# The ternary feed-forward of a two-layer network: its row parts and gelu outputs as two float32r parts instead of three bf16 parts, its square roots on GpSimd, its row normalisation on VectorE

## Chip, cores and metric

The kernel runs on one core of a Trainium2 chip. Times are device microseconds (us) of the whole kernel. The kernel before takes 2742.81 us, the median of 3 runs (2739.74 to 2743.94).

## What is computed

Sixteen sequences ("rows" of the work, b = 0 to 15) of 512 tokens and 256 features go through two layers, each an attention and a feed-forward with a residual. The change touches the last of the four stages, the ternary feed-forward, and the few lines at the end of the stage ahead of it that prepare its first row:

```python
def _ternary_linear(x, w):
    alpha = jnp.mean(jnp.abs(w))
    w_t = jnp.sign(w) * (jnp.abs(w) > 0.5 * alpha).astype(w.dtype)   # -1, 0 or 1
    rms = jnp.sqrt(jnp.sum(x * x, axis=-1, keepdims=True)) / jnp.sqrt(d)
    return jnp.einsum('bsd,fd->bsf', x / (rms + EPS), w_t)
h = jax.nn.gelu(_ternary_linear(layernorm(x), w_up), approximate=False)   # 256 -> 1024
x = x + _ternary_linear(h, w_down)                                        # 1024 -> 256
```

## The kernel before

One program for five engines, each with its own instruction order, tied by semaphores. The first attention ("ratio"), the low-rank feed-forward and the second attention ("zeroed") come first; `ternary_feed_forward` starts after all engines have met at the end of the second attention.

In this last stage x stays in SBUF. The work is 16 rows of `FC` = 8 slots; slot n is row b = n // 8 and block f = n % 8 of 128 hidden features, for all 512 tokens. The ternary weights lie in SBUF as bf16, where -1, 0 and 1 are exact. Float precision of the other operand comes from splitting it: a value is the sum of three bf16 parts, and a product is three bf16 matmuls that accumulate in one PSUM bank.

- **TensorE** (`pe`): `up(n)` does 2 feature halves x 3 parts = 6 matmuls with 512 moving columns (line 2237) into one of `H_BANKS` = 3 banks; `down(n)`, issued `T_LAG` = 3 slots later, does 4 token tiles x 3 parts = 12 matmuls (line 2248) whose stationary operand is a 128x128 tile of a gelu part and whose 256 moving columns are the weights. `turn_x` (line 119) transposes two token tiles of the next row in slots f = 1 and 4 (`T_TURN_AT`), 4 float32 transposes each, into the one `prep_bank`; `row_sums` (line 2259) in slot f = 7 adds the squares of the row before over partitions, into the same bank.
- **ScalarE** (`act`): in each slot `gelu` (2289, in place in PSUM), `high_part` (2294, the first bf16 part), `square` (2306). Beside them `keep_x` and `middle_x` (2280, 2285: parts 0 and 1 of the next row's x), once a row a square root for the hidden scale (2325), and once the roots for the late rows (2309, 2310). The root's function table and gelu's are loaded in turn, so each root costs two table loads.
- **VectorE** (`dve`): in each slot `split_rest` (2343: bank minus part 0), `split_mid` (2349: part 1) and `split_low` (2353: part 2). Beside them `split_x` (2336), `hidden_scale` (2359, 2361), and `finish` (2367), which adds a row's result to x in slots 0 and 1 of the row two later.
- **GpSimd** (`pool`): `normal` (2411: the next row's x normalised, two tiles at a time, at f = 0 and 2), the running sum of squares (2428, seven a row), `low_x` (2418: part 2 of x).

An up is released by the x parts of its row and by the bank of slot n - 3 being read (`h_rest`); a down by `h_lo`; a first down of a row by `x_added`, the finished x of the row two before, since down banks alternate in two pairs:

```python
q.wait_ge(s["h_rest"], n - H_BANKS + 1)                                # up(n)
q.wait_ge(s["h_lo"], n + 1)                                            # down(n)
q.wait_ge(s["x_added"], added(b - 2) if b >= 2 else 0)                 # down(n)
```

## Time and profile before

| | us |
|---|---|
| median of 3 runs (2739.74 to 2743.94) | 2742.81 |
| profiled execution, span from first to last instruction | 2743.6 |
| TensorE matmul busy in it | 2603.3 (95%) |
| VectorE, ScalarE, GpSimd busy | 2281.0, 2078.9, 1812.7 |

For the profiled execution the span is the only time that is shown; it lies 0.8 us over the median and inside the three runs. Lengths below are differences within this span. Busy shares are means over four stages of different kinds; the stage that the change touches is the last 377 us. Matmuls are pipelined, so the "mean ns of one" of a matmul includes the way through the array, and the distance between starts says what one costs in a stream.

### The profile page before, as it was taken

What the parts mean: (1) busy time and instruction counts of PE and PEld (TensorE: products, weight loads), DVE (VectorE), ACT (ScalarE), POOL (GpSimd) and SP (SyncE); (2) the same over time, 40 slices, a digit from 0 to 9 for tenths busy, and PEclk for the clock granted to TensorE, in tenths of its full rate; (3) what the DMA queues carried; (4) which work ended last, traced back from release to release, by engine and by line L of the source; (5) the groups of instructions that cost most, each with busy time, mean ns of one, the idle gap of its engine ahead of it and who ended that gap; (6) DMA issues with size and microseconds to landing.
All of it is one profiled execution on the core that took longest, in us unless ns stands there. A gap on an engine that the chain in (4) does not pass through costs nothing. (4 is left out here: it accounts for less than half of the span.)

```text
span 2743.6 us, 75250 instructions
## 1 busy us (share of the span) xinstructions
PE 2603.3 (95%) x27002; PEld 1814.6 (66%) x27044; DVE 2281.0 (83%) x6935; ACT 2078.9 (76%) x3788; POOL 1812.7 (66%) x3152
## 2 busy tenths in 40 slices
PE   5999999999999999999889999999999999899999
PEld 3777777777777777777333367777777767567666
DVE  5999999999999999988555588888888888599998
ACT  4998999998989999998334367677667676578886
POOL 4767666776677677766331177777777777578885
PEclk8999999999999999999989999999999999899999
DMA  4334433443343244322100256565655553000001
GB/s 121 72 60 76 76 61 63 81 81 63 63 81 71 54 75 81 70 49 46 41 1 20 50 100 104 97 101 99 104 102 99 101 96 66 1 16 24 24 24 39
DMA packets 110387, 182.21 MB, mean 66 GB/s; under 512 B 27008, under 2 KB 96384, under 8 KB 97920
## 3 DMA queue, kind: packets, MB, share of 16 engines
q1 hardware_dynamic: 106176, 175.82, 34.5%
q8 instruction: 216, 3.54, 0.6%
q10 hardware_dynamic: 3840, 1.58, 0.3%
q14 instruction: 155, 1.27, 0.2%
HBM read 116.25 MB, written 60.29 MB: 64 GB/s over the span
## 5 line engine op out<-in xcount | busy, mean ns | idle before, releaser
L922 POOL TENSOR_TENSOR ratio_scores<-ratio_scores,ratio_max_cols 128x512 f32<-128x512 f32 (+3 forms) x1024 | 726.3, 726 | 318.9 <-DVE ratio_max_cols L807 317.6
L198 PE MATMUL bank<-ratio_k_stack,ratio_q_stack 102*128 102x512 bf16 (+7 forms) x2048 | 506.1, 303 | 32.9 <-DVE ratio_max_cols L807 18.6
L1486 DVE CUSTOM_DVE_ANT_0 zeroed_unused<-bank,zeroed_drop 128x512 bf16<-128x512 f32 (+3 forms) x1024 | 439.7, 484 | 107.6 <-PE bank L198 107.6
L807 DVE CUSTOM_DVE_ANT_0 ratio_scores<-bank,ratio_scores 128x512 f32<-128x512 f32 (+3 forms) x1024 | 472.5, 489 | 22.2
L1362 ACT ACTIVATE arena<-bank 128x512 f32<-128x512 f32 x640 | 370.4, 593 | 150.3 <-PE bank L1255 148.9
L656 ACT ACTIVATE ratio_prob<-bank 128x512 f32<-128x512 f32 x640 | 378.8, 592 | 103.9 <-PE bank L554 101.1
L797 DVE TENSOR_TENSOR ratio_scores<-bank,ratio_inverse 128x512 f32<-128x512 f32 x640 | 435.9, 681 | 16.3 <-PE bank L198 9.6
L551 PE MATMUL bank<-const_f_sb,ratio_scores 128*128 128x128 f32 x2560 | 410.0, 274 | 0.9 <-ACT ratio_prob L656 0.9
L645 ACT ACTIVATE ratio_inverse<-bank 128x512 f32<-128x512 f32 x640 | 381.1, 596 | 12.0 <-PE bank L201 12.0
L649 ACT ACTIVATE ratio_inverse<-ratio_inverse 128x1024 f32<-128x1024 f32 x320 | 338.7, 1058 | 10.1
L1621 POOL TENSOR_SCALAR_AFFINE_SELECT arena<-arena 128x256 f32<-128x256 f32 (+1 forms) x640 | 227.9, 362 | 164.3 <-ACT arena L1362 159.9
L551 PEld LDWEIGHTS bank<-const_f_sb,ratio_scores 128*128 128x128 f32 x2560 | 301.6, 141 | 42.1 <-issue 1.9
L198 PEld LDWEIGHTS bank<-ratio_k_stack,ratio_q_stack 96*128 96x128 bf16 (+1 forms) x2048 | 179.0, 98 | 192.6 <-DVE ratio_max_cols L807 110.5
L1255 PE MATMUL bank<-zeroed_q_stack,zeroed_k_stack 99*128 99x128 bf16 x2560 | 249.8, 219 | 11.5 <-ACT arena L1362 10.8
L198 PE MATMUL bank<-zeroed_k_stack,zeroed_q_stack 96*128 96x512 bf16 (+3 forms) x1024 | 248.0, 305 | 2.8 <-PEq L2163 2.1
L1255 PEld LDWEIGHTS bank<-zeroed_q_stack,zeroed_k_stack 99*128 99x128 bf16 x2560 | 178.1, 97 | 91.3 <-ACT arena L1362 56.0
L554 PE MATMUL bank<-const_b_sb 128*128 128x128 bf16 x1024 | 211.9, 219 | 0.0
L2428 POOL TENSOR_TENSOR ternary_square_sum<-ternary_square_sum,ternary_squares 128x512 f32<-128x512 f32 x112 | 151.0, 1348 | 73.4 <-ACT ternary_squares L2306 70.7
L201 PE MATMUL bank<-const_b_sb 128*128 128x128 bf16 x1024 | 193.1, 220 | 0.0
L2248 PE MATMUL bank<-ternary_w_down_T,ternary_h_parts 128*128 128x256 bf16 x1536 | 189.1, 273 | 2.2 <-DVE ternary_h_parts L2353 2.2
L1961 ACT ACTIVATE lowrank_hidden<-bank,lowrank_b 128x512 f32<-128x512 f32 x128 | 82.2, 685 | 135.0 <-PE bank L1843 135.0
L2248 PEld LDWEIGHTS bank<-ternary_w_down_T,ternary_h_parts 128*128 128x128 bf16 x1536 | 150.3, 98 | 47.8 <-DVE ternary_h_parts L2353 4.3
(223 smaller groups left out, 5436.3 us busy)
## 6 DMA issues: line engine op xcount, KB each, us to landing
ratio_q_stack<-ratio_parts_q SPq DMA_DIRECT2D x186, 128.0 KB
ratio_k_stack<-ratio_parts_k SPq DMA_DIRECT2D x186, 128.0 KB
zeroed_q_stack<-zeroed_parts_q SPq DMA_DIRECT2D x186, 128.0 KB, 4.5
zeroed_k_stack<-zeroed_parts_k SPq DMA_DIRECT2D x186, 128.0 KB, 7.4
ratio_parts_q<-arena SPq DMA_DIRECT2D x96, 128.0 KB
ratio_parts_k<-arena SPq DMA_DIRECT2D x96, 128.0 KB
zeroed_parts_q<-shared_parts SPq DMA_DIRECT2D x96, 128.0 KB
zeroed_parts_k<-shared_parts SPq DMA_DIRECT2D x96, 128.0 KB
```

The source lines that it names most:

```text
L198: i = e.matmul(bank[:, off:off + w], qs[0:rows, s, hh, ib * P:(ib + 1) * P], ks[0:rows, s, hh, 0:w], start=(k == 0), stop=mask is None, sk ...
L551: e.matmul(bank[:, at], scores[:, n % S_BUFS, at], net.ident, is_transpose=True, start=first, stop=False, skip_group_check=True)
L645: e.activation(inv[:, n % INV_BUFS, :], shared("denoms", n)[:, :], ACT.Ln, scale=-2.0, bias=EPS_RATIO).then_inc(s["log_den"])
L649: e.activation(both, both, ACT.Exp, scale=-1.0).then_inc(s["inverse"])
L656: e.activation(prob[:, n % PROB_BUFS, 0:wd], exp_banks[n % 2][:, 0:wd], ACT.Exp).then_inc(s["prob"])
L797: e.tensor_tensor(scores[:, n % S_BUFS, 0:wd], dot_banks[n % 2][:, 0:wd], inv[:, n % INV_BUFS, 0:wd], ALU.mult).then_inc(s["weighed"])
L807: i = e.tensor_tensor_reduce(seg, dot_banks[n % 2][:, at], seg, 1.0, 0.0, ALU.mult, ALU.max, mx[:, pair % M_BUFS, c:c + 1])
L922: i = e.tensor_tensor(seg, seg, mx[:, pair % M_BUFS, c:c + 1].to_broadcast([P, w]), ALU.subtract)
L1255: i = e.matmul(bank[:, off + jb * P:off + (jb + 1) * P], ks[0:STACK + FOLD_ROWS, st, hh, jb * P:(jb + 1) * P], qs[0:STACK + FOLD_ROWS, st, ...
L1362: e.activation(prob[:, n % FOLD_PROBS, 0:wd], exp_banks[n % 2][:, 0:wd], ACT.Exp, scale=0.25).then_inc(s["prob"])
L1486: i = e.tensor_tensor_reduce(unused[:, n % 2, at], bank[:, at], drop[:, L - (ib + 1) * P:L], 1.0, 0.0, ALU.add, ALU.max, mx[:, pair % FOLD ...
L2248: i = e.matmul(banks[t // 2][:, (t % 2) * D:(t % 2 + 1) * D], h_parts[:, n % H_BUFS, part, t * P:(t + 1) * P], ternary.down[:, f, :], star ...
```

## The change

In the last stage every three-part bf16 product becomes a two-part float32r product: x parts and h parts are float32r tensors `[P, 2, 2, L]` and `[P, H_BUFS, 2, L]`; an up is 4 matmuls, a down 8. The weights are copied once, at the start of the stage, from bf16 to float32r: eight copies by VectorE (`up_w`), eight by GpSimd (`down_w`). The middle parts and the rests go away; VectorE's part of a slot is one subtraction (`low_part`). VectorE also takes `normal` (from GpSimd) and `keep_x` (from ScalarE). The square roots are GpSimd's `pow` with 0.5, after a small VectorE operation that reads PSUM (`hidden_mean`); ScalarE keeps gelu, high part and square. `finish` and `hidden_scale` go to slots 0 and 1. The last bank wait of an up is now for `h_lo` and `h_squared`. At the end of the stage ahead, the first row's x is split in two parts instead of three. Of the diff, without the functions that only changed engine or were removed:

```diff
-        self.parts = sb("shared_parts", [P, 2, 3, L], BF16)
-        self.rest = sb("shared_rest", [P, L])
-        self.x_parts = self.parts[:, :, :, :].rearrange("p a b t -> p (a b t)").rearrange("p (k c t) -> p k c t", k=3, c=2)
-        self.x_rest = self.rest[:, :].rearrange("p (c t) -> p c t", c=2)
+        sb("shared_block", [P, 4 * L])
+        base = nc.sbuf_base - 16 * L
+        self.parts = nc.alloc_sbuf_tensor_at("shared_parts", [P, 2, 3, L], BF16, offset=base)
+        self.rest = nc.alloc_sbuf_tensor_at("shared_rest", [P, L], F32, offset=base + 12 * L)
+        self.x_parts = nc.alloc_sbuf_tensor_at("ternary_first_parts", [P, 2, 2, L], F32R, offset=base)
...
-            def first_rest(pair):
+            def first_low(pair):
                 q.wait_ge(ts["x_hi"], pair + 1)
-                q.wait_ge(ts["x_lo"], pair)
                 q.wait_ge(s["lo"], 2 * halves)
-                e.tensor_tensor(rows.x_rest, prep_bank[:, :].rearrange("p (c t) -> p c t", c=2), x_part(pair, 0),
-                                ALU.subtract).then_inc(ts["x_rest"])
+                e.tensor_tensor(x_part(pair, 1), prep_bank[:, :].rearrange("p (c t) -> p c t", c=2), x_part(pair, 0),
+                                ALU.subtract).then_inc(ts["x_lo"])
...
-        xn, x_rest = start.xn, start.x_rest
-        x_parts = (start.x_parts, sb("x_parts", [P, 3, 2, L], BF16))
-        h_parts = sb("h_parts", [P, H_BUFS, 3, L], BF16)
-        h_rest = sb("h_rest", [P, 2, L])
+        up_w = sb("up_wide", [P, 2, F], F32R)
+        down_w = sb("down_wide", [P, FC, D], F32R)
+        xn = start.xn
+        x_parts = (start.x_parts, sb("x_parts", [P, 2, 2, L], F32R))
+        h_parts = sb("h_parts", [P, H_BUFS, 2, L], F32R)
         sq = sb("squares", [P, 2, L])
         total = sb("square_sum", [P, 2, L])
         hs = sb("h_scale", [P, 2, T])
+        half = sb("half", [P, B * T - start.rows])
...
             def turn_x(b, pair):
                 q.wait_ge(s["xn"], 2 * b + pair + 1)
-                q.wait_ge(s["x_rest"], 2 * b + pair)
+                q.wait_ge(s["x_lo"], 2 * b + pair)
                 if pair == 0:
-                    q.wait_ge(s["h_rms"], b - 2)
+                    q.wait_ge(s["h_mean"], b - 2)
                 turn_blocks(e, prep_bank, lambda t: xn[:, t % 2, :], pair, net.ident).then_inc(s["turned"])
 
             def up(n):
                 b, f = divmod(n, FC)
+                if b == 0:
+                    q.wait_ge(s["up_wide"], f + 1)
                 q.wait_ge(s["x_lo"], 2 * b + 2)
-                q.wait_ge(s["h_rest"], n - H_BANKS + 1)
+                q.wait_ge(s["h_lo"], n - H_BANKS + 1)
+                q.wait_ge(s["h_squared"], n - H_BANKS + 1)
                 for c in range(2):
-                    for part in range(3):
-                        i = e.matmul(h_banks[n % H_BANKS][:, :], ternary.up[:, c, f * P:(f + 1) * P], x_parts[b % 2][:, part, c, :],
-                                     start=(c == 0 and part == 0), stop=(c == 1 and part == 2))
+                    for part in range(2):
+                        i = e.matmul(h_banks[n % H_BANKS][:, :], up_w[:, c, f * P:(f + 1) * P], x_parts[b % 2][:, part, c, :],
+                                     start=(c == 0 and part == 0), stop=(c == 1 and part == 1))
                 i.then_inc(s["up"])
 
             def down(n):
                 b, f = divmod(n, FC)
                 banks = down_banks[2 * (b % 2):2 * (b % 2) + 2]
+                if b == 0:
+                    q.wait_ge(s["down_wide"], f + 1)
+                q.wait_ge(s["h_hi"], n + 1)
                 q.wait_ge(s["h_lo"], n + 1)
                 q.wait_ge(s["x_added"], added(b - 2) if b >= 2 else 0)
                 for t in range(T):
-                    for part in range(3):
+                    for part in range(2):
                         i = e.matmul(banks[t // 2][:, (t % 2) * D:(t % 2 + 1) * D],
-                                     h_parts[:, n % H_BUFS, part, t * P:(t + 1) * P], ternary.down[:, f, :],
-                                     start=(f == 0 and t % 2 == 0 and part == 0), stop=(f == FC - 1 and part == 2),
+                                     h_parts[:, n % H_BUFS, part, t * P:(t + 1) * P], down_w[:, f, :],
+                                     start=(f == 0 and t % 2 == 0 and part == 0), stop=(f == FC - 1 and part == 1),
                                      skip_group_check=True)
                 i.then_inc(s["down"])
...
             def row_sums(b):
                 q.wait_ge(s["h_summed"], (b + 1) * (FC - 1))
-                q.wait_ge(s["h_rms"], b)
-                q.wait_ge(s["x_rest"], min(2 * (b + 3), 2 * B))
+                q.wait_ge(s["h_mean"], b)
+                q.wait_ge(s["x_lo"], min(2 * (b + 3), 2 * B))
                 for t in range(T):
...
-            for n in range(n_slots + FC):
-                b, f = divmod(n, FC)
-                if n < n_slots:
-                    gelu(n)
-                    high_part(n)
-                    square(n)
-                if b + 1 < B and f in T_TURN_AT:
-                    keep_x(b + 1, T_TURN_AT.index(f))
-                if b + 1 < B and f in T_PARTS_AT:
-                    middle_x(b + 1, T_PARTS_AT.index(f))
-                if b and f == T_SUMS_AT:
-                    q.wait_ge(s["h_rows"], b)
-                    q.wait_ge(s["x_added"], added(b - 3) if b >= 3 else 0)
-                    e.activation(hs[:, (b - 1) % 2, :], prep_bank[:, 0:T], ACT.Sqrt, scale=1.0 / F).then_inc(s["h_rms"])
-                if n == ROOTS_AT:
-                    roots()
+            for n in range(n_slots):
+                gelu(n)
+                high_part(n)
+                square(n)
...
+            def keep_x(b, pair):
+                q.wait_ge(s["turned"], 2 * b + pair + 1)
+                q.wait_ge(s["up"], (b - 1) * FC)
+                e.tensor_copy(x_part(b, pair, 0), prep_bank[:, :].rearrange("p (c t) -> p c t", c=2)).then_inc(s["x_hi"])
+
             def low_x(b, pair):
-                q.wait_ge(s["x_mid"], 2 * b + pair + 1)
-                q.wait_ge(s["up"], (b - 1) * FC)
-                e.tensor_tensor(x_part(b, pair, 2), x_rest[:, :, :], x_part(b, pair, 1), ALU.subtract).then_inc(s["x_lo"])
-
-            for n in range(n_slots):
+                q.wait_ge(s["x_hi"], 2 * b + pair + 1)
+                e.tensor_tensor(x_part(b, pair, 1), prep_bank[:, :].rearrange("p (c t) -> p c t", c=2), x_part(b, pair, 0),
+                                ALU.subtract).then_inc(s["x_lo"])
+
...
+            def low_part(n):
+                q.wait_ge(s["h_hi"], n + 1)
+                q.wait_ge(s["h_squared"], n + 1)
+                e.tensor_tensor(h_parts[:, n % H_BUFS, 1, :], h_banks[n % H_BANKS][:, :], h_parts[:, n % H_BUFS, 0, :],
+                                ALU.subtract).then_inc(s["h_lo"])
+
+            def hidden_mean(b):
+                q.wait_ge(s["h_rows"], b + 1)
+                e.tensor_scalar(hs[:, b % 2, :], prep_bank[:, 0:T], 1.0 / F, None, ALU.mult).then_inc(s["h_mean"])
+
...
+            for f in range(FC):
+                e.tensor_copy(up_w[:, :, f * P:(f + 1) * P], ternary.up[:, :, f * P:(f + 1) * P]).then_inc(s["up_wide"])
+            for n in range(n_slots + 2 * FC):
                 b, f = divmod(n, FC)
+                if n < n_slots:
+                    low_part(n)
                 if b + 1 < B and f in T_XN_AT:
                     normal(b + 1, T_XN_AT.index(f))
-                if f:
+                if b + 1 < B and f in T_KEEP_AT:
+                    keep_x(b + 1, T_KEEP_AT.index(f))
+                    low_x(b + 1, T_KEEP_AT.index(f))
+                if 0 < b <= B and f == T_SUMS_AT:
+                    hidden_mean(b - 1)
+                if n == SCALES_AT:
+                    scales()
+                if 2 <= b < B + 2 and f == 0:
+                    hidden_scale(b - 2)
+                if 2 <= b < B + 2 and f < 2:
+                    finish(b - 2, 2 * f)
+                    finish(b - 2, 2 * f + 1)
+
...
+            def roots():
+                variance = net.mean_var[:, start.rows:B * T, 1]
+                e.tensor_scalar(scale[:, :], variance, 1e-5, None, ALU.add).then_inc(s["std_in"])
+                q.wait_ge(s["halves"], 1)
+                e.tensor_tensor(rms[:, :], variance, half[:, :], ALU.pow).then_inc(s["std"])
+                q.wait_ge(s["std_in"], 1)
+                e.tensor_tensor(scale[:, :], scale[:, :], half[:, :], ALU.pow).then_inc(s["std"])
+
+            def hidden_root(b):
+                out = hs[:, b % 2, :]
+                q.wait_ge(s["h_mean"], b + 1)
+                q.wait_ge(s["halves"], 1)
+                e.tensor_tensor(out, out, half[:, 0:T], ALU.pow).then_inc(s["h_rms"])
+
+            e.memset(half[:, :], 0.5).then_inc(s["halves"])
+            for f in range(FC):
+                e.tensor_copy(down_w[:, f, :], ternary.down[:, f, :]).then_inc(s["down_wide"])
+            for n in range(n_slots + FC):
+                b, f = divmod(n, FC)
+                if n < n_slots and f:
                     q.wait_ge(s["h_squared"], n + 1)
                     if f > 1:
                         q.wait_ge(s["h_summed"], summed(n) - 1)
                     e.tensor_tensor(total[:, b % 2, :], total[:, b % 2, :], sq[:, n % 2, :], ALU.add).then_inc(s["h_summed"])
-                if b + 1 < B and f in T_PARTS_AT:
-                    low_x(b + 1, T_PARTS_AT.index(f))
+                if b and f == T_SUMS_AT:
+                    hidden_root(b - 1)
+                if n == ROOTS_AT:
+                    roots()
```

TensorE's order from the row sums at the end of row 1 to the first transposes (`L119`) in slot 1 of row 2. Before:

```order
L2259 MATMUL bank<-const_f_sb,ternary_square_sum 128x1 x4
L2237 MATMUL bank<-shared_parts,ternary_w_up_T 128x512 x6
L2248 MATMUL bank<-ternary_w_down_T,ternary_h_parts 128x256 x12
L2237 MATMUL bank<-shared_parts,ternary_w_up_T 128x512 x6
L2248 MATMUL bank<-ternary_w_down_T,ternary_h_parts 128x256 x12
L119 MATMUL bank<-const_f_sb,shared_xn 128x128 x4
```

Now, at the same place (`L120` is the same helper one line later, `ternary_first_parts` the x parts of even rows):

```order
L2255 MATMUL bank<-const_f_sb,ternary_square_sum 128x1 x4
L2230 MATMUL bank<-ternary_first_parts,ternary_up_wide 128x512 x4
L2244 MATMUL bank<-ternary_down_wide,ternary_h_parts 128x256 x8
L2230 MATMUL bank<-ternary_first_parts,ternary_up_wide 128x512 x4
L2244 MATMUL bank<-ternary_down_wide,ternary_h_parts 128x256 x8
L120 MATMUL bank<-const_f_sb,shared_xn 128x128 x4
```

The order of ups, downs and transposes stays; only the number of matmuls in each falls by a third.

VectorE's order in slots 0 to 2 of row 12. Before (`L2343`, `L2353`, `L2349` are the three splits of gelu's output, the middle one of them for the slot before):

```order
L2343 TENSOR_TENSOR ternary_h_rest<-bank,ternary_h_parts 128x512
L2353 TENSOR_TENSOR ternary_h_parts<-ternary_h_rest,ternary_h_parts 128x512
L2349 CAST ternary_h_parts<-ternary_h_rest 128x512
L2367 SCALAR_TENSOR_TENSOR x<-bank,ternary_h_scale,x 128x256 x2
L2343 TENSOR_TENSOR ternary_h_rest<-bank,ternary_h_parts 128x512
L2353 TENSOR_TENSOR ternary_h_parts<-ternary_h_rest,ternary_h_parts 128x512
L2349 CAST ternary_h_parts<-ternary_h_rest 128x512
L2367 SCALAR_TENSOR_TENSOR x<-bank,ternary_h_scale,x 128x256 x2
```

Now, from the low part of slot 0 (`L2326`) on; `L2309` normalises two token tiles of row 13, `L2316` and `L2320` are their two parts, `L2344` is `finish`:

```order
L2326 TENSOR_TENSOR ternary_h_parts<-bank,ternary_h_parts 128x512
L2309 TENSOR_SCALAR shared_xn<-x,mean_var,ternary_x_scale 128x256 x2
L2336 TENSOR_SCALAR ternary_h_scale<-ternary_h_scale 128x4
L2338 RECIPROCAL ternary_h_scale<-ternary_h_scale 128x4
L2344 SCALAR_TENSOR_TENSOR x<-bank,ternary_h_scale,x 128x256 x2
L2326 TENSOR_TENSOR ternary_h_parts<-bank,ternary_h_parts 128x512
L2344 SCALAR_TENSOR_TENSOR x<-bank,ternary_h_scale,x 128x256 x2
L2326 TENSOR_TENSOR ternary_h_parts<-bank,ternary_h_parts 128x512
L2309 TENSOR_SCALAR shared_xn<-x,mean_var,ternary_x_scale 128x256 x2
L2316 CAST ternary_x_parts<-bank 128x2x256
L2320 TENSOR_TENSOR ternary_x_parts<-bank,ternary_x_parts 128x2x256
```

A slot of VectorE has one operation instead of three, and the normalisations, which were GpSimd's, now stand behind the low parts of slots 0 and 2. GpSimd's order per row is seven sums of squares and one `pow`.

## Rows read from the trace of the kernel before

**Rows 1.** Head of the page: span, and busy time of each engine.
```profile
span 2743.6 us, 75250 instructions
PE 2603.3 (95%) x27002; PEld 1814.6 (66%) x27044; DVE 2281.0 (83%) x6935; ACT 2078.9 (76%) x3788; POOL 1812.7 (66%) x3152
```
**Rows 2.** Busy time by windows: stretch, length, each engine, clock, DMA share, GB/s.
```profile
2366.60:2413.10 46.50, 42.08 (x263) 27.17 (x269) 36.13 (x48) 31.47 (x56) 34.77 (x25) 0.93 0.00 1
...
2435.90:2731.80 295.90, 292.52 (x2050) 206.19 (x2083) 266.04 (x419) 238.22 (x402) 235.69 (x164) 1.00 0.07 24
```
**Rows 3.** Waits of PE from 2413 us on: total, times, longest.
```profile
PE bank L2248 <- DVE ternary_h_parts L2353: 1.3, 2, 1.1
PE bank L2237 <- POOL ternary_x_parts L2418: 1.3, 3, 0.9
```
**Rows 4.** Timeline of PE, a steady slot: start, length, engine, line, operation, count.
```profile
2590.15 1.47 PE L2248 MATMUL bank<-ternary_w_down_T,ternary_h_parts 128*128 128x256 bf16 x12
2591.46 1.46 PE L2237 MATMUL bank<-ternary_x_parts,ternary_w_up_T 128*128 128x512 bf16 x6
2592.75 1.47 PE L2248 MATMUL bank<-ternary_w_down_T,ternary_h_parts 128*128 128x256 bf16 x12
```
**Rows 5.** Timeline of PE: the first and the fifteenth of the sixteen row sums.
```profile
2413.12 0.95 PE L2259 MATMUL bank<-const_f_sb,ternary_square_sum 128*128 128x1 f32 x8
...
2731.84 0.95 PE L2259 MATMUL bank<-const_f_sb,ternary_square_sum 128*128 128x1 f32 x8
```
**Rows 6.** Timeline of PE in earlier stages: float32 products and transposes.
```profile
300.91 1.94 PE L576 MATMUL bank<-ratio_w_o,arena 128*128 128x256 f32 x8
...
1291.49 0.60 PE L563 MATMUL bank<-const_f_sb,ratio_o_group 128*128 128x128 f32 x4
```
**Rows 7.** One line's instructions, ns min/median/max: weight loads, float32 and bf16.
```profile
L525 PEld LDWEIGHTS bank<-ratio_w_in,arena x512: 186/192/333, 27.1 to 1244.0; 128*128 128x128 f32 x171
...
L2248 PEld LDWEIGHTS bank<-ternary_w_down_T,ternary_h_parts x1536: 95/98/181, 2374.7 to 2736.8; 128*128 128x128 bf16 x192
```
**Rows 8.** Timeline of ACT where it runs without a wait.
```profile
2417.91 0.59 ACT L2306 ACTIVATE ternary_square_sum<-bank 128x512 f32<-128x512 f32 x1
2418.39 0.60 ACT L2289 ACTIVATE bank<-bank 128x512 f32<-128x512 f32 x1
2419.02 0.60 ACT L2294 ACTIVATE ternary_h_parts<-bank 128x512 bf16<-128x512 f32 x1
2419.52 0.59 ACT L2306 ACTIVATE ternary_squares<-bank 128x512 f32<-128x512 f32 x1
```
**Rows 9.** Timeline around one slot: down, next gelu, square, subtraction.
```profile
2502.04 1.47 PE L2248 MATMUL bank<-ternary_w_down_T,ternary_h_parts 128*128 128x256 bf16 x12
2502.24 0.58 ACT L2289 ACTIVATE bank<-bank 128x512 f32<-128x512 f32 x1 [0.91 <-PE bank L2237]
...
2503.35 0.59 ACT L2306 ACTIVATE ternary_squares<-bank 128x512 f32<-128x512 f32 x1
...
2504.08 0.68 DVE L2343 TENSOR_TENSOR ternary_h_rest<-bank,ternary_h_parts 128x512 f32<-128x512 f32 x1
```
**Rows 10.** Groups by line and shape: busy us, mean ns of one.
```profile
L2343 DVE TENSOR_TENSOR ternary_h_rest<-bank,ternary_h_parts 128x512 f32<-128x512 f32 x128 | 87.7, 685 | 42.5 <-ACT ternary_square_sum L2306 31.4 <-ACT ternary_squares L2306 6.2 <-issue 3.6
L2367 DVE SCALAR_TENSOR_TENSOR x<-bank,ternary_h_scale,x 128x256 f32<-128x256 f32 x64 | 27.7, 477 | 0.0
L1988 DVE COPY lowrank_xn_T<-bank 128x512 f32<-128x512 f32 x16 | 11.0, 690 | 15.8 <-PE bank L119 15.8
L1456 DVE TENSOR_SCALAR shared_xn<-x,mean_var,rstd 128x256 f32<-128x256 f32 x60 | 24.3, 448 | 0.0
L1601 POOL TENSOR_SCALAR zeroed_neg_max<-zeroed_max_cols 128x8 f32<-128x8 f32 x128 | 31.6, 247 | 6.4 <-DVE zeroed_max_cols L1486 6.4
L2428 POOL TENSOR_TENSOR ternary_square_sum<-ternary_square_sum,ternary_squares 128x512 f32<-128x512 f32 x112 | 151.0, 1348 | 73.4 <-ACT ternary_squares L2306 70.7
```
**Rows 11.** Timeline, start of the stage: first up, first transposes.
```profile
2367.09 3.71 PE L2237 MATMUL bank<-shared_parts,ternary_w_up_T 128*128 128x512 bf16 x11 [2.50 <-PEq L1695]
...
2370.64 0.60 PE L119 MATMUL bank<-const_f_sb,shared_xn 128*128 128x128 f32 x4
```
**Rows 12.** Timeline, end of the stage: the last root and the last finish.
```profile
2738.00 0.17 ACT L2325 ACTIVATE ternary_h_scale<-bank 128x4 f32<-128x4 f32 x1 [4.08 <-PE bank L2259]
...
2738.62 1.66 DVE L2367 SCALAR_TENSOR_TENSOR x<-bank,ternary_h_scale,x 128x256 f32<-128x256 f32 x4
```

90 lines of the change are left out of this document (22 added, 68 removed).

## Prediction

> **What bounds the kernel now.** I read the head of the page first [rows 1]: TensorE is busy 95% of the span and no other engine over 83%. That is a mean over four stages, so the second view is the busy time by windows for the stage that the change touches [rows 2]: from 2435.90 to 2731.80 us, thirteen of its rows, TensorE's matmuls are busy 292.5 of 295.9 us, VectorE 266, ScalarE 238, GpSimd 236, at the full clock (granted 1.00, the 2.4 GHz level). Third, TensorE's waits from 2413 us on [rows 3]: they sum to about 3 us. So in this stage TensorE is the bound by its own work, and every other engine waits for it.
>
> What a slot costs is read from starts [rows 4]: down starts at 2590.15, up at 2591.46, down at 2592.75. So 12 matmuls of 256 columns take 1.31 us (0.109 each) and 6 of 512 columns 1.29 us (0.215 each): one column in a cycle of the 2.4 GHz clock, plus 2 ns. A slot is 2.60 us. Fourteen rows lie between the two row sums of [rows 5]: (2731.84 - 2413.12) / 14 = 22.77 us a row, of which 8 x 2.60 = 20.8 are slots, two groups of transposes (0.44 each by their pitch of 0.11) and one of row sums (0.8) make 1.7, and 0.3 is jitter.
>
> **Part 1, the products.** A third of the matmuls goes. What a float32r matmul costs, no row shows. The bounds from both sides: the bf16 rows (0.109 and 0.215 us [rows 4]), since one instruction with one weight load cannot stream faster than a column a cycle; and the float32 rows. A float32 product is two instructions of two cycles a column each: eight instructions of 256 columns in 1.94 us, less the last one's way through the array, are 0.223 each [rows 6], twice bf16. The four column times of a float32 product are what two halves times two halves cost, and a float32r product drops the lower halves, so one product of the four is left, and I take the bf16 pace of one column a cycle. The float32 pace would make the slot 3.57 us (rival B). The Trainium skill (FP8 and Floating Point Precision, "TensorE Precision Notes") says the same of "FP32 reduced precision", an operand cut to about 22 bits, against 4 passes for true FP32.
>
> The weight load is the second unknown, since a down loads 128x128 float32 values for only 256 columns. Float32 loads are listed with 192 ns and bf16 loads with 98 [rows 7], but these include latency: the eight row sums of one column each [rows 5] take 0.95 us with the last one's 0.25, so (0.95 - 0.25) / 7 = 0.10 us is what a float32 load costs in a stream. That is under the 0.109 of the columns, and float32 transposes of 128 columns keep a pitch of (0.60 - 0.27) / 3 = 0.11 [rows 6] with a load each, so loads do overlap columns. I take 0.112 for a down matmul and 0.215 for an up: down 8 x 0.112 = 0.90, up 4 x 0.215 = 0.86, slot 1.76 instead of 2.60. Gain: 8 x 0.84 = 6.7 us a row.
>
> The Trainium skill (TensorE: Matmul & The Clock Gate, Part 3, "The mechanism") has a rule against this change: a weight load overlaps running matmuls only when the row groups differ. Here all rows are used, and the trace disagrees: 12 bf16 pairs of load (98 ns) and 256 columns run at 0.109. It is rival C below, for float32r alone.
>
> **Part 2, who can follow a slot of 1.76 us.** ScalarE without waits starts square, gelu, high part, square at 2417.91, 2418.39, 2419.02, 2419.52 [rows 8]: 1.61 us a slot, and keep_x, middle_x and all table loads leave it. It just holds. GpSimd: seven sums of 1.27 to 1.35 us [rows 10] are 9.4 a row and the pow, against some 17. VectorE a row: 8 low parts of 0.69, 4 normalisations of 0.41 to 0.45, two copies of 0.69, two subtractions of 0.69, 4 finishes of 0.48 [rows 10], some 0.6 of small ones: 12.3 us, 72%. So TensorE stays the bound by sum. But order matters: normalisations now queue behind low parts.
>
> Let t = 0 be the end of up(8b). Gelu starts 0.20 later, the square ends at 1.9 [rows 9], the low part at 2.65, the two normalisations at 3.45. TensorE does down, up, down (0.90 + 0.86 + 0.90) and stands at the transposes at 2.66: **a new stall of 0.8 us** in every row, where GpSimd had normalised ahead of the slot. With the later chain (finish x4, low parts, second normalisation behind the low part of slot 2 at about 7.4, then the first pair's copy and subtraction until 9.6) the second transposes, which wait for that subtraction to free the bank, are due at 9.2: another 0.4. The up after the second pair, x parts for the next row, has over 1 us to spare. Finish of the row two before ends at 6.3, due at 6.5 for the first down of a row: just free. Should GpSimd's sum hold a normalisation back, 0.5 more; that goes to the range. Stalls: 1.2 us a row.
>
> **Row after:** 22.77 - 6.72 + 1.2 = 17.25; 14 rows x 5.5 = **77 us** gained.
>
> **Part 3, the ends.** Rows 0 and 1 up to the first row sums have 16 ups and 13 downs: 16 x 0.43 + 13 x 0.41 = 12.2 gained, less two rows' stalls (2.4). At the start the first transposes came 3.55 us after the first up [rows 11]; they now wait for VectorE's eight weight copies (some 0.3 us each, beside TensorE's first ups), the low part of slot 0 and the normalisations, some 6 us, so 2.5 lost; 7 left. At the end three downs of 0.41 less, the root now through VectorE and GpSimd with two more hops against 0.17 [rows 12]: +1 us gained net. The pow has no row; a GpSimd operation on 8 columns takes 0.25 [rows 10], and the other bound is open; up to about 3 us it is hidden in a row, since it starts behind the sum of slot 7 and its result is used behind the low part and the normalisations of the next slot 0. I take it as hidden, and at 0.5 at the end. The split of the first row at the end of the stage ahead loses two steps of 0.6 and 1.2 us beside other work: 0. Table loads of ScalarE lie in its idle time: 0.
>
> **Sum:** 77 + 7 + 1 = 85. Against the profiled execution 2743.6 - 85 = 2658.6; the median lies 0.8 lower: **2658 us**. The case's own range: no stall at all would be 2658 - 18 = 2640 or, with the start smooth too, 2634; a down pitch of 0.125 and 0.8 us more stall a row 2658 + 13 + 13 = 2684.
>
> **Rivals.**
> A. *The load paces the downs.* If a float32r load takes the 0.19 us that the record lists, a down is 8 x 0.19 = 1.52, a slot 2.38, the gain 0.22 x 128 = 28 and no stall is left, since TensorE comes to the transposes at 3.9: 2743 - 28 = **2715**. Against it: the 0.10 of the row sums.
> B. *Slower: float32r streams at the pace of each float32 instruction*, two cycles a column. Every 4-byte matmul in this trace does, the single-instruction transposes too (0.11 for 128 columns). Down 8 x 0.223 = 1.78, up 4 x 0.446 = 1.78, slot 3.57 against 2.60: +124 on TensorE, **2867**. It decides as soon as a column costs over 1.5 cycles, where 2/3 of the columns cost as much as before. Each product issued as two instructions, like plain float32, would be +580; a small part of this chance.
> C. *Loads in series with columns*: down 8 x (0.109 + 0.10), up 4 x (0.215 + 0.10), slot 2.93, +0.33 x 128 = 42: **2785**.
> D. *VectorE becomes the bound.* Normalisations that GpSimd's sums hold up (the shortest is 0.41, means reach 0.45 with little beside) or a pow over 3 us: a row of 20 instead of 17.25, 14 x 2.8 = 39 given back: **2697**.
> E. *It does nothing*: the bf16 matmuls are really gone from TensorE's order, so only by coincidence.
>
> **Chances.** Forecast case 0.71, A 0.08, B 0.08, C 0.03, D 0.08, E and the rest 0.02. What a measurement tells from no change is about 0.2%, 5.5 us. Faster 0.87 (forecast, A, D), same 0.02, slower 0.11. The range 2632 to 2712 holds nearly all of the forecast case and D; it leaves out B, C and most of A.
>
> **What would show it.** Right: in the steady rows 8 float32r matmuls start within 0.9 us and 4 within 0.87, a row sum every 17 us, TensorE's waits at the transposes for VectorE's xn about 0.8 us, fifteen times, ScalarE near 75 to 80% in the stage, each pow under 3 us. Wrong: a down pitch of 0.19 (A) or 0.22 (B), ups of 1.8 us (B), TensorE busy as before, or long waits of the downs for finished x or of VectorE for a root (D).

## The result, and the profile after

The changed kernel takes **2662.3 us** (median of 4 runs, 2658.9 to 2663.9), against 2742.6 (4 runs of the kernel before on the same chip, 2739.7 to 2743.9): ratio 0.9705, 95% interval 0.9691 to 0.9720. It is faster by 80 us; 2658 was forecast. The runs further down were made on other chips, where the kernel before took 2743.8 to 2748.4 (medians by chip); so times of two kernels that lie less than some 5 us apart are not told apart here.

The head of the page of the kernel after, beside [rows 1]:

```profile
span 2660.9 us, 73392 instructions
PE 2514.8 (95%) x26276; PEld 1807.2 (68%) x26276; DVE 2135.9 (80%) x6793; ACT 2003.7 (75%) x3679; POOL 1693.0 (64%) x3088
```

TensorE lost 88 us of work and is at 95% as before; every other engine lost work too. Busy time by windows, from the first row sum on (stretch, length, PE, PEld, DVE, ACT, POOL, clock, DMA share, GB/s), beside [rows 2]:

```profile
2398.90:2650.00 251.10, 240.74 (x1572) 216.20 (x1571) 158.07 (x320) 187.85 (x338) 145.70 (x117) 1.00 0.09 30
```

VectorE fell from 90% of the stretch to 63%, GpSimd from 80% to 58%, ScalarE from 81% to 75%; TensorE is at 96%: it has no matmul under way for about 10 us, a wait being counted there only from the modelled end of the last one. The timeline of PE, one piece of a steady row, beside [rows 4]:

```profile
2475.08 1.11 PE L2244 MATMUL bank<-ternary_down_wide,ternary_h_parts 128*128 128x256 f32 x8
2476.59 0.66 PE L120 MATMUL bank<-const_f_sb,shared_xn 128*128 128x128 f32 x4 [0.40 <-DVE shared_xn L2309]
2477.01 1.17 PE L2230 MATMUL bank<-ternary_first_parts,ternary_up_wide 128*128 128x512 f32 x4
2478.01 1.10 PE L2244 MATMUL bank<-ternary_down_wide,ternary_h_parts 128*128 128x256 f32 x8
2478.95 1.10 PE L2230 MATMUL bank<-ternary_first_parts,ternary_up_wide 128*128 128x512 f32 x4
2479.89 1.12 PE L2244 MATMUL bank<-ternary_down_wide,ternary_h_parts 128*128 128x256 f32 x8
...
2481.78 1.11 PE L2244 MATMUL bank<-ternary_down_wide,ternary_h_parts 128*128 128x256 f32 x8
2483.24 0.63 PE L120 MATMUL bank<-const_f_sb,shared_xn 128*128 128x128 f32 x4 [0.34 <-DVE ternary_x_parts L2320]
```

Starts of down, up and down (2478.01, 2478.95, 2479.89): 0.94 us for each step, a slot of 1.88 instead of 2.60. A down matmul starts 0.119 us after the one ahead and an up 0.232 (medians of the starts in the trace; the bf16 ones before stood at 0.109 and 0.216). The two gaps are the new stalls: eight downs from 2475.08 are through at 2475.08 + 8 x 0.119 = 2476.03, the transposes start 0.56 later; the second group comes 0.51 late in the same way.

The row sums, beside [rows 5]:

```profile
2398.92 0.95 PE L2255 MATMUL bank<-const_f_sb,ternary_square_sum 128*128 128x1 f32 x8
...
2648.88 0.95 PE L2255 MATMUL bank<-const_f_sb,ternary_square_sum 128*128 128x1 f32 x8
```

(2648.88 - 2398.92) / 14 = **17.85 us a row**, 22.77 before, 17.25 forecast. PE's waits from 2400 us on, beside [rows 3]:

```profile
PE bank L120 <- DVE shared_xn L2309: 5.3, 13, 0.4
PE bank L120 <- DVE ternary_x_parts L2320: 2.9, 7, 1.0
PE bank L120 <- DVE ternary_first_parts L2320: 2.1, 6, 0.4
```

All of them are at the transposes (line 120), the place that the prediction named. On VectorE the chain behind the first stall, with the pow on GpSimd:

```profile
2473.66 1.02 POOL L2395 TENSOR_TENSOR ternary_h_scale<-ternary_h_scale,ternary_half 128x4 f32<-128x4 f32 x1
...
2475.20 0.69 DVE L2326 TENSOR_TENSOR ternary_h_parts<-bank,ternary_h_parts 128x512 fp32r<-128x512 f32 x1 [2.00 <-ACT ternary_square_sum L2292]
2475.81 0.73 DVE L2309 TENSOR_SCALAR shared_xn<-x,mean_var,ternary_first_scale 128x256 f32<-128x256 f32 x2
...
2480.62 1.14 DVE L2309 TENSOR_SCALAR shared_xn<-x,mean_var,ternary_first_scale 128x256 f32<-128x256 f32 x2
```

Before 2475.20 VectorE was idle for 2.00 us with the normalisations waiting behind that low part in its queue. The pow was done by 2474.68, and is in nobody's way.

Where the 82.7 us between the two spans (2743.6 and 2660.9) came from:

| stretch | before | after | gain |
|---|---|---|---|
| up to the first up (2367.09, 2363.52) | 2367.1 | 2363.5 | 3.6 |
| first up to the first row sums | 46.0 | 35.4 | 10.6 |
| 14 rows | 318.7 | 250.0 | 68.8 |
| last full row to the end | 11.8 | 12.0 | -0.3 |

The first line can't be put down to the change: over the kernels below, whose stages ahead are all but the same, the first up came anywhere from 2358.7 to 2372.4.

### The profile page after: what moved, and what is told of

It reads as the page before. It is cut to its first block and busy times, and to the rows that moved or that the text cites. A ratio compares the mean times of both kernels' runs of the same rounds, so it can differ in the third digit from the quotient of the medians.

```text
span 2660.9 us, 73392 instructions
## 1 busy us (share of the span) xinstructions
PE 2514.8 (95%) x26276; PEld 1807.2 (68%) x26276; DVE 2135.9 (80%) x6793; ACT 2003.7 (75%) x3679; POOL 1693.0 (64%) x3088
## 5 line engine op out<-in xcount | busy, mean ns | idle before, releaser
L1258 PE MATMUL bank<-zeroed_q_stack,zeroed_k_stack 99*128 99x128 bf16 x2560 | 249.7, 219 | 11.7 <-ACT arena L1365 10.6
L2406 POOL TENSOR_TENSOR ternary_square_sum<-ternary_square_sum,ternary_squares 128x512 f32<-128x512 f32 x112 | 144.8, 1293 | 121.3 <-ACT ternary_squares L2292 120.9
L214 PE MATMUL bank<-arena,zeroed_v_ones 128*32 128x128 f32 x5120 | 179.4, 276 | 0.9
L214 PE MATMUL bank<-ratio_prob,ratio_v_ones 128*32 128x128 f32 x5120 | 179.4, 276 | 0.0
```

The costliest lines, as they stand in the source:

```text
L214: i = e.matmul(o_bank[32 * h:32 * h + 32, ib * P:(ib + 1) * P], values_ones[:, vs, jb, (g % 2) * GROUP + h, :], prob[:, (base + u) % bufs, ...
L1258: i = e.matmul(bank[:, off + jb * P:off + (jb + 1) * P], ks[0:STACK + FOLD_ROWS, st, hh, jb * P:(jb + 1) * P], qs[0:STACK + FOLD_ROWS, st, ...
```

## Theories and experiments

Two things take the place of what the products gave up: the pitch of float32r, over the bf16 pace that was assumed, and the two stalls a row, which come from the order on VectorE. The rival accounts are that the moves of work between engines made the gain, that some engine other than TensorE now sets the pace, and that the weight load does. In each expectation T1 and T2 are stated anew.

**bf16 parts in place of float32r.** The changed kernel with bf16 parts, weights and products. It keeps two of the three bf16 parts, so the third part's share of every product is left out.

```diff
-        up_w = sb("up_wide", [P, 2, F], F32R)
-        down_w = sb("down_wide", [P, FC, D], F32R)
+        up_w, down_w = ternary.up, ternary.down
...
-        h_parts = sb("h_parts", [P, H_BUFS, 2, L], F32R)
+        h_parts = sb("h_parts", [P, H_BUFS, 2, L], BF16)
...
```

> The changed kernel with bf16 in place of float32r: two bf16 parts, the bf16 weights used directly, no weight copies. It leaves the third bf16 part out of both products. Theory 1 (the element type itself costs: in the changed kernel a 256-column float32r matmul is started every 0.119 us against 0.109 for bf16, a 512-column one every 0.232 against 0.216): the slot falls from 1.88 to 1.74 us, 8 x 0.14 = 1.1 us a row; TensorE then comes earlier to the transposes and gives 0.3 to 0.6 of that back as longer waits for VectorE; 16 rows x 0.5 to 0.8 = 8 to 13 us faster than the changed kernel, about 2651 us. Theory 2 (the pace of the matmuls is set by traffic or by the number of loads, not the type): pitches stay at 0.119 and 0.232, time stays at 2662.

Measured: 2654.8 us, ratio 0.9672 (0.9653 to 0.9691). The slot is 1.74 us (pitches 0.109 and 0.216), the row 17.18: of 8 x 0.14 = 1.1 us less on TensorE only 0.67 arrived. The rest went into longer stalls, as this wait of the transposes shows (0.68 us, where the changed kernel has 0.34; timeline of PE of this kernel):

```profile
2481.61 0.63 PE L120 MATMUL bank<-const_f_sb,shared_xn 128*128 128x128 f32 x4 [0.68 <-DVE ternary_x_parts L2315]
```

**Normalisations ahead of the low part**, on VectorE:

```diff
+                if b + 1 < B and f in T_XN_AT:
+                    normal(b + 1, T_XN_AT.index(f))
                 if n < n_slots:
                     low_part(n)
-                if b + 1 < B and f in T_XN_AT:
-                    normal(b + 1, T_XN_AT.index(f))
```

> The changed kernel with one exchange in VectorE's order: the normalisation of the next row's tiles stands ahead of the slot's low part instead of behind it. Theory 1 (the first wait of a row at the transposes, 0.57 us from the end of the down's columns, and 1.8 us in the first row are the normalisation queued behind the low part): both go, 15 x 0.57 + 1.8 = 10 us less than the changed kernel, 2652; the second wait of a row (0.52) stays, since it hangs on the first pair's two parts. Theory 2 (TensorE would wait there anyway for GpSimd's or ScalarE's work, or what is saved comes back at the next bank wait): under 3 us, 2660 to 2662.

Measured: 2644.4 us, ratio 0.9631 (0.9615 to 0.9648). No wait of PE is left from 2400 us on, and its timeline runs through the transposes:

```profile
2482.66 1.11 PE L2244 MATMUL bank<-ternary_down_wide,ternary_h_parts 128*128 128x256 f32 x8
2483.61 0.60 PE L120 MATMUL bank<-const_f_sb,shared_xn 128*128 128x128 f32 x4
```

The transposes start 0.95 us behind the down ahead of them, which is a down's own length, and so does the second group (2488.70 and 2489.65). The row is 16.73 us, which is 8 x 1.88 of slots and 1.7 of transposes and row sums. 14 x 1.12 = 15.7 us come from the rows and 4.1 from the start of the stage (31.3 instead of 35.4), 19.8 together, against 19.7 between the spans. More than expected: the second stall, which was to stay, went with this one edit too. The edit moves the normalisations of both slots, so it doesn't tell which of the two moves freed the second group. The start had the same queue, and something more: behind its wait of 1.81 us there the changed kernel ran for a few us at half the clock (the row of the windows stands further down), and without that wait the granted clock stays at 1.00 from 2367 us on.

**The copies and subtractions of x ahead too** (`keep_x` and `low_x` before `low_part` as well):

> As the run before, and also the two parts of the next row's x ahead of the low part in slots 2 and 5. Theory 1: the second wait (0.52 us a row, for the bank that the first pair's parts free) goes too: 15 x (0.57 + 0.52) + 1.8 = 18 us less than the changed kernel, 2644. Theory 2 (low parts that now stand behind these hold back downs and ups): the second wait turns into one on the low part, 2652 or more.

Measured: 2640.8 us, ratio 0.9629 (0.9599 to 0.9658), a row of 16.72. Three of its four runs lie a few us under those of the edit before and one over them, and the row is the same, so that is no difference: with TensorE never waiting, nothing is left for VectorE's order to give.

**Both at once**: two bf16 parts (the third left out) and the normalisations ahead.

> The kernel with bf16 parts and products, two of the three parts (the third is left out), with the normalisations ahead of the low part: the fourth corner of a square with the changed kernel, the bf16 kernel and the one with the normalisations ahead. T1, the two losses of the changed kernel are separate, pitch 0.119 and 0.232 against 0.109 and 0.216 (0.98 us a row by the slots) and the stalls at the transposes: both are gone here, the row is 8 x 1.74 + 0.9 + 0.8 = 15.6 us, 14 x 1.1 = 16 us less than with the normalisations ahead alone, about 2627 us. T2, at a slot of 1.74 us ScalarE (1.61 us a slot without waits) or VectorE paces the row, and stalls return: no better than 2640 us.

Measured: 2624.2 us, ratio 0.9569 (0.9542 to 0.9597), a row of 15.59. The four kernels make a square, in us a row:

| | low part first | normalisations first | stalls |
|---|---|---|---|
| float32r | 17.85 | 16.73 | 1.12 |
| bf16 | 17.18 | 15.59 | 1.59 |

Without stalls the pitch is worth 1.14, what eight slots of 1.88 against 1.74 give; with them, 0.67. And ScalarE, at 1.61 us a slot, still follows one of 1.74.

**The moves alone.** The kernel before, with its three bf16 parts and all its products, but normalisation and the copies of x on VectorE and the roots as a pow on GpSimd. Of the edit, what comes into VectorE's loop:

```diff
+                if b + 1 < B and f in T_XN_AT:
+                    normal(b + 1, T_XN_AT.index(f))
                 if b + 1 < B and f in T_SPLIT_AT:
+                    keep_x(b + 1, T_SPLIT_AT.index(f))
                     split_x(b + 1, T_SPLIT_AT.index(f))
...
```

> The kernel before with everything of the change but the products: three bf16 parts as before, normalisation and first x part on VectorE, roots by GpSimd's pow, finish and scale in the changed kernel's slots. Theory 1 (the whole gain is the third of the matmuls; the rest moved work that was hidden): TensorE's slot stays 2.60 us, so no gain at all; VectorE gets 8 x (0.69 + 1.03 + 0.68) = 19.2 by the means of the kernel before, plus 4 x 0.41, 2 x 0.69, 2 x 0.68, 4 x 0.48 and 0.5 = 26 us a row, 24 if GpSimd disturbs it less, against 22.8: slower by 14 x 1.2 to 3.2 = 17 to 45 us, 2760 to 2788. Theory 2 (the moves gained something by themselves, for instance by the table loads that go): under 2742.

Measured: 2764.7 us in one run, against a median of 2746.3 for the kernel before on that chip: 18 us **slower**. A row is 23.77 us, 1.0 more than before. The waits of PE (2420 to 2730 us) are at the same transposes and at the next row's first up:

```profile
PE bank L2238 <- POOL ternary_x_parts L2414: 4.3, 7, 1.0
PE bank L2238 <- POOL shared_parts L2414: 3.4, 6, 0.7
PE bank L119 <- DVE shared_xn L2322: 3.1, 13, 0.2
```

VectorE is busy 269.0 of 286.4 us in it (2440.6 to 2727.0), 94% where the kernel before has 90%. So with three parts the moves gain nothing and cost, and the gain has to come from the products. What the moves are worth beside two-part products is another question. The products alone, with every other piece of work left where it was, were not run; the two kernels that follow each take one move back:

**The roots back on ScalarE**, all else as in the changed kernel:

```diff
+                if b and f == T_SUMS_AT:
...
+                    e.activation(hs[:, (b - 1) % 2, :], prep_bank[:, 0:T], ACT.Sqrt, scale=1.0 / F).then_inc(s["h_rms"])
...
```

> The changed kernel with the square roots back on ScalarE, as before the change: one Sqrt a row in slot 7 behind the square, with a load of the root's table and one of gelu's (1.28 us each); GpSimd's pow and VectorE's scaling ahead of it go. Theory 1 (with a slot of 1.88 us ScalarE has 0.27 us to spare in each, so 2.7 us more in one place are seen): the next gelu is 2.5 us late, so the low part of slot 0 and the normalisation behind it, and TensorE's wait at the first transposes grows from 0.57 to about 3 us: 15 x 2.4 = 36 us slower than the changed kernel, 2698. Theory 2 (three banks of gelu and the idle time of ScalarE hide the loads, as they did before): 2662 to 2668.

Measured: 2693.7 us, ratio 0.9811 (0.9789 to 0.9832), 31 us slower than the changed kernel and near the 2698 of Theory 1. Timelines of ACT and PE of this kernel around one root:

```profile
2479.76 1.28 ACT L2307 ACT_TABLE_LOAD   x1
2481.06 0.17 ACT L2307 ACTIVATE ternary_h_scale<-bank 128x4 f32<-128x4 f32 x1
2481.25 1.28 ACT L2275 ACT_TABLE_LOAD   x1
...
2485.74 1.07 PE L120 MATMUL bank<-const_f_sb,shared_xn 128*128 128x128 f32 x4 [2.14 <-DVE shared_xn L2321]
2486.46 2.06 PE L2230 MATMUL bank<-ternary_first_parts,ternary_up_wide 128*128 128x512 f32 x4
```

Two table loads and the root are 2.7 us of ScalarE ahead of the next gelu. The square, the low part and the normalisations follow from that gelu, so the listed wait grew from 0.4 to 2.1 us. And here it cost more than itself: the transposes after it took 1.07 us instead of 0.66, the ups 2.06 instead of 1.17. The busy time by windows (columns as in the result) behind this wait and behind the same wait of the row after show the clock:

```profile
2485.70:2489.00 3.30, 3.26 (x12) 2.88 (x13) 2.49 (x7) 0.60 (x2) 1.28 (x1) 0.52 0.00 0
2506.60:2509.90 3.30, 3.28 (x20) 2.95 (x21) 2.48 (x7) 1.76 (x4) 1.29 (x1) 1.00 0.00 0
```

The first ran near the 1.2 GHz level, the second at 2.4 GHz, behind waits of 2.14 and 2.13 us. Of the thirteen such waits from 2400 us on nine were followed by a stretch at half the clock and four were not; a row with such a stretch is 20.7 to 20.9 us and one without it 19.7 to 20.0; 20.23 is the mean. The pow of 1.02 us on GpSimd removes all that; only at the end of the kernel does it cost 1.7 us (12.0 against 10.4 from the fifteenth row sums on).

**The normalisations back on GpSimd**, ahead of its sum:

> The changed kernel with the normalisation back on GpSimd, ahead of its sums in slots 0 and 2. Theory 1 (the move to VectorE was not needed for the gain): GpSimd has 7 x 1.29 + 1.02 + 4 x 1.2 to 1.5 = 15 to 16 us in a row of 17.8, starts the pair before the low part, and the first wait at the transposes goes: 15 x 0.57 = 8 us less, 2654. Theory 2 (GpSimd comes late: its operation for the pair of slot 2 ends 3 us after it starts, sums behind it hold ScalarE's squares, and VectorE's operations that share SBUF with it are held): slower than the changed kernel, 2665 to 2690.

Measured: 2673.1 us, ratio 0.9734 (0.9712 to 0.9756), 11 us slower than the changed kernel. A pair takes 2.45 us on GpSimd (0.73 on an undisturbed VectorE), behind the pow in its queue, and the transposes wait about 1 us in each row. A steady row is 18.0 us all the same, as in the changed kernel (17.95), since there is one wait of 1 us in it instead of two of 0.4. So Theory 2 has the time right, but not by what it says of every row. One row took 24.8, and the timelines of POOL and PE say why:

```profile
2411.59 2.31 POOL L2374 TENSOR_TENSOR ternary_x_rms<-mean_var,ternary_half 128x12 f32<-128x12 f32 x1
2413.85 2.28 POOL L2376 TENSOR_TENSOR ternary_x_scale<-ternary_x_scale,ternary_half 128x12 f32<-128x12 f32 x1
2416.11 2.45 POOL L2385 TENSOR_SCALAR shared_xn<-x,mean_var,ternary_first_scale 128x256 f32<-128x256 f32 x2
...
2418.61 1.11 PE L120 MATMUL bank<-const_f_sb,shared_xn 128*128 128x128 f32 x4 [5.85 <-POOL shared_xn L2385]
```

The two pows of 12 columns for the late rows' roots, 4.6 us, stand in the same queue, and the transposes, behind a wait of 5.85 us, took 1.11 us instead of 0.66 (granted clock 0.67 from 2418.5 to 2425.0). That one row is the whole loss that the trace shows in the rows: 6.9 us. The two spans differ by 15.7 us, and the other 8.9 lie ahead of the first up, where nothing was changed. So the move of the normalisations to VectorE is worth that one row as it stands in the change, and 1.2 us in each row once they go ahead of the low part there (16.73). With the pow on GpSimd, nothing that TensorE waits for soon should stand behind it.

**What paces a float32r matmul.** Three kernels issue each down matmul of 256 columns in pieces, with a load for each, and one does so in bf16:

```diff
-                    for part in range(2):
+                    for part, c in ((0, 0), (0, P), (1, 0), (1, P)):
...
```

> The changed kernel with each down matmul of 256 columns split into two of 128, with the same stationary operand loaded for each. Theory 1 (a float32r matmul of few columns is paced by its weight load, about 0.11 to 0.12 us, as float32 transposes of 128 columns are): 16 x 0.115 = 1.84 us for a down, slot 2.77, 0.9 x 128 = 115 us slower than the changed kernel minus the waits that go (16): about 2760. Theory 2 (load and columns are in series for float32r): 16 x (0.11 + 0.056) = 2.7, +220, 2880. Theory 3 (narrow float32r matmuls fall to the float32 pace of four column times, 0.21 us or more): 16 x 0.22 = 3.5, slot 4.4, +330, 2990.

> The changed kernel with each down matmul of 256 columns issued as two, of 64 and of 192 columns (one more weight load for each; the ups as they are). T1, a float32r down waits for its weight load of about 0.11 us whenever its columns take less, and streams a column in a cycle: the 64-column one starts its successor after 0.11 us, the 192-column one after 0.11 too; a down step is 16 x 0.111 = 1.78 us, the same as with two halves of 128, and the row 23.4 us. T2, narrow float32r matmuls take two cycles for a column: 64 columns 0.056 us and 192 columns 0.16, a step of 8 x 0.216 = 1.73 us; the starts tell them apart even where the sums do not.

> The changed kernel with each down matmul of 256 columns issued as four of 64. T1, every float32r matmul waits for its own weight load of 0.11 us: 64 columns start 0.11 apart, a down step is 32 x 0.111 = 3.55 us, a row 17.85 + 8 x 2.61 less the 1.1 us of stalls = 37.6 us, some 3015 us. T2, a float32r matmul of under 256 columns takes two cycles for a column, and the load hides behind them: 64 columns start 0.053 to 0.056 apart, a step is 1.71 to 1.79 us and the row 23 to 23.5 us, as with halves of 128 and with pieces of 64 and 192, about 2745 us.

> The kernel with two bf16 parts (the third left out) and the normalisations ahead, with each down matmul of 256 columns issued as two of 128. T1, the two-cycle rate of narrow matmuls is float32r's own: here 128 columns start 0.055 us apart, the slot stays 1.74 us and the time near 2624 us. T2, narrow matmuls are slow because a weight load takes about 0.1 us whatever the type: 128 columns start 0.098 to 0.11 apart, a row is 8 x 0.8 = 6.5 us longer, some 2720 us.

Measured, one run each: 2748.5 us in halves of 128, 2750.5 in pieces of 64 and 192, **3466.4** in four of 64, 2628.3 for the bf16 kernel in halves of 128. Timelines of PE, a down step and what follows it: first of the halves, then of the pieces of 64 and 192 (one group of 16, named by its first).

```profile
2480.37 1.90 PE L2245 MATMUL bank<-ternary_down_wide,ternary_h_parts 128*128 128x128 f32 x16
2482.10 0.62 PE L120 MATMUL bank<-const_f_sb,shared_xn 128*128 128x128 f32 x4
```

```profile
2478.44 1.93 PE L2245 MATMUL bank<-ternary_down_wide,ternary_h_parts 128*128 128x64 f32 x16
2480.20 0.60 PE L120 MATMUL bank<-const_f_sb,shared_xn 128*128 128x128 f32 x4
```

The weight loads of that same step (15 of the 16 are in the record):

```profile
2478.45 1.75 PEld L2245 LDWEIGHTS bank<-ternary_down_wide,ternary_h_parts 128*128 128x128 f32 x15
```

Of the four pieces of 64 columns, a step at the full clock and one at half of it:

```profile
2384.10 3.77 PE L2245 MATMUL bank<-ternary_down_wide,ternary_h_parts 128*128 128x64 f32 x32
2387.68 2.06 PE L2230 MATMUL bank<-ternary_first_parts,ternary_up_wide 128*128 128x512 f32 x4
2389.53 6.87 PE L2245 MATMUL bank<-ternary_down_wide,ternary_h_parts 128*128 128x64 f32 x32
```

And of the bf16 halves:

```profile
2480.43 1.06 PE L2240 MATMUL bank<-ternary_w_down_T,ternary_h_parts 128*128 128x128 bf16 x16
2481.33 1.03 PE L2227 MATMUL bank<-ternary_x_parts,ternary_w_up_T 128*128 128x512 bf16 x4
```

Per matmul that is 1.73 / 16 = 0.108, 1.76 / 16 = 0.110 and 3.58 / 32 = 0.112 us: the same for 128, for 64 and 192, and for 64 columns. Two cycles for a narrow column would have given 0.053 for the last one. So a float32r weight load costs 0.11 us at the 2.4 GHz level and matmuls that are shorter wait for it; of the widths tried only 256 and 512 columns cover it (0.119 and 0.232 us a matmul). A bf16 load hides under 128 columns (0.90 / 16 = 0.056). The pieces of 64 and 192 alone left this open: their sum was that of two loads, but the trace's starts stood 0.052 and 0.172 us apart in turns, which neither theory had, and which looked like two cycles a column. The loads of that step do stand evenly: 15 of them in 1.75 us, the last one listed with 0.19, is (1.75 - 0.19) / 14 = 0.111 from start to start. That also speaks against a fixed cost of 0.11 for each float32r matmul as such, since the matmuls themselves start 0.052 apart. No kernel here kept one load for several matmuls, which would settle it outright, and why the matmuls' starts are uneven stays open.

The Trainium skill (TensorE: Matmul & The Clock Gate, "Weight-path perf modes — Fast Weight Load (FWL) and DoubleRow") says that fast weight load is on for 128 weights unless the input is FP32. It doesn't name float32r; if float32r counts as FP32 there, its load is the slow kind, and 0.11 against at most 0.056 us agrees.

The kernel in four pieces lost 450 us more than the load explains. Busy time by windows of its stage:

```profile
2440.00:3300.00 860.00, 860.00 (x3817) 821.66 (x3818) 148.65 (x294) 167.07 (x301) 130.22 (x104) 0.52 0.02 8
```

TensorE is listed as busy without a gap and the granted clock is 0.52, near the 1.2 GHz level; the row is 69.0 us where 37.6 was expected. What the engine did before the clock fell was a stream of matmuls with 64 columns to a load. The kernels in halves and in pieces of 64 and 192, whose loads come at the same 0.11 us, kept a granted clock of 1.00 from 2400 to 2730 us. This is one run, so how steadily it comes isn't known.

## Why the prediction was right

**Part 1, the products**: right in kind, its gain put a sixth too high. The float32r matmuls run at nearly one column a cycle, so the bf16 pace was the right choice and rival B did not come. The term that was off is the pitch: 0.119 and 0.232 us against the 0.112 and 0.215 that I took, a slot of 1.88 instead of 1.76, so 8 x 0.72 = 5.8 us a row and not 6.7, or 13 us over the 14 rows. I had named a down pitch of 0.125 as the bound, but gave the ups no bound above bf16. The load was read nearly right from the row sums: 0.10, where the starts of those row sums in the trace stand 0.112 apart but for the first, and a float32r load takes 0.111. So it is not under the 0.109 of 256 bf16 columns, as the prediction says, but just over it, and the 0.112 that was taken for a down is the load's own pace. The measured 0.119 is above both. What adds the rest to a down, and 0.016 to an up, isn't settled: for the up, at 0.232, the load is far from the pace. That a float32r product is a quarter of a float32 one was an argument from how the halves multiply; the runs bear out its pace and not the reason.

**Part 2, the stalls**: place, cause and size held. Stalls of 0.56 and 0.51 us stand at the two groups of transposes, 1.1 us a row, against 0.8 and 0.4. The first is shorter since TensorE comes later to it: down, up and down are 0.95 + 0.93 + 0.95 = 2.83 us and not 2.66. That the normalisations, queued behind the low part, are the cause is shown by the edit that swaps them. The second stall had a part that the prediction left to its range: the second pair took 1.14 us instead of 0.73, beside a GpSimd sum.

**Row after**: 17.85 against 17.25, gain 68.8 us and not 77. The smaller gain of the products adds 0.96 us to a row, the shorter stalls take 0.1 off again, and about 0.2 more goes off by rows that aren't like the others: the first two of the fourteen were 1.2 and 0.9 us longer than the rest in the kernel before, and the last one, which has no transposes, has no stalls after the change.

**Part 3, the ends**: +10.6 instead of 7 at the start, by errors that went both ways. The products gave 29 x 0.36 = 10.4 and not 12.2. The first transposes came 5.3 us after the first up (3.55 before), so 1.75 us were lost there and not 2.5:

```profile
2363.52 3.48 PE L2230 MATMUL bank<-ternary_first_parts,ternary_up_wide 128*128 128x512 f32 x8 [2.46 <-DVE ternary_up_wide L2360]
2368.82 0.66 PE L120 MATMUL bank<-const_f_sb,shared_xn 128*128 128x128 f32 x4 [1.81 <-DVE shared_xn L2309]
```

The larger miss is a wait of the kernel before that I never priced, since I read the waits only from 2413 us on. Its timeline of PE, a little earlier:

```profile
2389.95 2.34 PE L2237 MATMUL bank<-ternary_x_parts,ternary_w_up_T 128*128 128x512 bf16 x5 [2.88 <-POOL ternary_x_parts L2418]
2392.07 2.10 PE L2248 MATMUL bank<-ternary_w_down_T,ternary_h_parts 128*128 128x256 bf16 x12
```

It waited 2.88 us for GpSimd's third part of x, and the matmuls behind ran slower (a down step of 1.94 us from start to start instead of 1.31). The changed kernel has no third part, and no such wait. The slower matmuls are half the clock again, and both kernels have such a stretch, the one before behind this wait and the changed one behind its 1.81 us, so that they about cancel (busy time by windows, of the kernel before, then of the changed kernel; the third number from the end is the granted clock):

```profile
2389.90:2394.20 4.30, 4.25 (x18) 2.34 (x18) 2.15 (x5) 1.67 (x3) 4.27 (x3) 0.60 0.00 0
2369.90:2373.40 3.50, 3.50 (x13) 2.92 (x12) 0.86 (x2) 2.60 (x5) 1.29 (x2) 0.51 0.00 0
```

The end gained nothing (-0.3, forecast +1): the two pows there are 1.02 and 1.01 us where I took 0.5, with two hops each. In the rows the pow is hidden, as assumed. Another 3.6 us came from the stage ahead, which is chance; without them the gain would be 79, against the 85 forecast. So the median came as near as 4 us in part by luck: the rows were 8 us short, and two things that the prediction didn't have, the old wait of 2.88 us and the 3.6 from ahead of the stage, made up for most of it.

**Rivals.** A: the downs start at 0.119, not 0.19; but its mechanism is real, and a tile half as wide meets it (2748 us, the whole gain). C: load and columns in series would be 0.209 for a down, and it is 0.119. D: VectorE has 37% of the stretch free, and the pow isn't near 3 us; the pows of 12 columns are at 2.3 each, and the normalisations were no longer in their queue.

## What to carry to other kernels

Two float32r parts in place of three bf16 ones paid here with 256 and 512 columns behind each weight load, and lost the whole gain with 128; count 0.12 us for 256 columns and 0.23 for 512. When the bound engine gets faster, look at the queue order of its suppliers first: what it waits for soonest goes ahead of what is due a slot later, which here was worth another 18 us (2644 against 2662) for swapping two lines. A root once a row was better on an engine that needs no table loads (31 us here), as long as nothing urgent is queued behind it. And a wait of TensorE is to be priced with the clock behind it: look at the granted clock of the few us behind it, and in more than one row.

## What was not expected of the hardware

A float32r matmul is not quite at bf16 pace: 0.119 against 0.109 us for 256 columns, 0.232 against 0.216 for 512. A float32r weight load costs 0.11 us and a bf16 load at most 0.056, though the record lists 190 and 98 ns, so a listed load length is 1.7 times its price or more. GpSimd's pow grows with the columns: 1.02 us for 128x4, 2.3 for 128x12. The same wait of 2.13 us was followed by a stretch at half the clock in nine rows of thirteen and not in the other four. Elsewhere a wait of 1.81 us was followed by it (the changed kernel, 2368.82), while one of 1.79 us (the kernel with two bf16 parts, 2371.30) and one of 3.40 us (the moves alone, 2395.07) were not; none of the waits of up to 0.7 us in the steady rows was. So the length of a wait alone doesn't tell, and what does isn't settled here. And in one run a gapless stream of float32r matmuls with 64 columns to a load went at a granted clock of 0.52 for a whole stage.
